# Expert weights in the memory of the mixed values, the second attention's weights loaded beside the routing, and new positions for its parts

## What is computed

```python
x = x + 0.5 * L0_ffn(layernorm(x))     # 8 small experts, every token through all, weights of the best 2
x = x + L0_attn(layernorm(x))          # 32 heads of 32, then a layernorm of its output
x = x + 0.5 * L0_ffn(layernorm(x))
x = x + 0.5 * L1_ffn(layernorm(x))     # 8 large experts, each takes its best 640 tokens (routing by rank)
x = x + L1_attn(layernorm(x))          # 16 heads of 64, with biases
x = x + 0.5 * L1_ffn(layernorm(x))
```

## Time and profile before

| | us |
|---|---|
| median of 3 runs | 3257.68 (3253.45 to 3260.6) |
| the profiled execution's own time | 3266.09 |
| its span in the trace | 3264.3 |
| PE busy | 2913.5 (89% of the span) |
| DVE busy | 2133.6 (65%) |
| POOL busy | 1748.0 (54%) |
| ACT busy | 1720.8 (53%) |

### The profile page before, as it was taken

How to read it: one execution, slowest core, us unless ns; L and a number is a source line. 1 busy time by engine, 2 the same in 40 slices (tenths; PEclk the granted TensorE clock), 3 DMA queues, 4 the chain that set the end, 5 groups by cost and what they waited for, 6 DMA issues and landing times. The chain is left out here.

```text
span 3264.3 us, 46697 instructions
## 1 busy us (share of the span) xinstructions
PE 2913.5 (89%) x16106; PEld 1945.8 (60%) x16106; DVE 2133.6 (65%) x4522; ACT 1720.8 (53%) x3308; POOL 1748.0 (54%) x1540
## 2 busy tenths in 40 slices
PE   7999999999999999989936759999999999998176
PEld 7984565555555555478825736656656566565175
DVE  5667776777777677657765337676676766766632
ACT  5656776767777676757612314444444444443033
POOL 0006988889898888911104714444444444444066
PEclk9999999999999999999967969999999999999588
DMA  2004433434443343300002344344443444432034
GB/s 94 1 20 98 98 88 90 98 80 97 93 93 89 81 97 87 77 5 21 21 30 60 64 114 111 89 104 96 101 104 89 103 93 101 102 89 57 26 76 76
DMA packets 182988, 254.00 MB, mean 78 GB/s; under 512 B 35904, under 2 KB 75584, under 8 KB 182208
## 3 DMA queue, kind: packets, MB, share of 16 engines
q1 hardware_dynamic: 168672, 240.19, 31.1%
q0 software_dynamic: 14080, 10.82, 2.5%
HBM read 33.44 MB, written 16.67 MB: 15 GB/s over the span
## 5 line engine op out<-in xcount | busy, mean ns | idle before, releaser
L1761 POOL TENSOR_TENSOR arena<-arena 128x512 f32<-128x512 f32 x1152 | 1443.5, 1280 | 767.3 <-ACT arena L1132 743.7
L789 PE MATMUL psum<-stack 96*128 96x512 f32 (+4 forms) x4096 | 1247.3, 434 | 37.1 <-DVE top L1391 15.5
L1132 ACT ACTIVATE arena<-psum 128x512 f32<-128x512 f32 x1536 | 854.7, 599 | 604.9 <-PE psum L789 600.4
L1391 DVE TENSOR_REDUCE top<-psum 128x1 f32<-128x512 f32 x1536 | 981.8, 677 | 171.8 <-PE psum L789 169.5
L789 PEld LDWEIGHTS psum<-stack 96*128 96x128 f32 (+4 forms) x4096 | 716.3, 191 | 440.3 <-issue 217.8
L819 PE MATMUL psum<-arena,values 128*32 128x512 f32 (+1 forms) x3072 | 493.3, 598 | 0.5
L819 PEld LDWEIGHTS psum<-arena,values 128*32 128x32 f32 (+1 forms) x3072 | 132.3, 119 | 271.6 <-issue 230.5
L777 PE MATMUL psum<-xT,wqkv 128*128 128x512 f32 x512 | 270.4, 610 | 5.7 <-ACT xT L981 5.7
L1730 POOL TENSOR_SCALAR rstd<-mv 128x4 f32<-128x4 f32 x56 | 12.7, 227 | 473.1 <-DVE mv L1253 471.1
L1422 DVE RECIPROCAL psum<-psum 128x128 f32<-128x128 f32 x256 | 243.3, 954 | 18.6 <-PE psum L851 18.6
L689 PE MATMUL psum<-stack 128*128 128x512 f32 x768 | 213.3, 414 | 20.0 <-DVE stack L1290 20.0
(11 more groups left out here) (155 smaller groups left out, 3132.4 us busy)
## 6 DMA issues: line engine op xcount, KB each, us to landing
stack<-halves SPq DMA_DIRECT2D x768, 128.0 KB, 2.3
stack<-halves SPq DMA_DIRECT2D x384, 256.0 KB, 4.7
tokens<-xn SPq DMA_DIRECT2D x16, 256.0 KB, 2.5
sums<-X SPq DMA_DIRECT2D x16, 256.0 KB, 2.8
wqkv<-in_wg SPq DMA_DIRECT2D x16, 256.0 KB
wqkv<-in_wu SPq DMA_DIRECT2D x16, 256.0 KB
wqkv<-in_wd SPq DMA_DIRECT2D x16, 256.0 KB
wqkv<-in_w_qkv SPq DMA_DIRECT2D x2, 1536.0 KB, 9.6
```

Source lines behind the costliest of these rows:

```text
L789: ins = T_.matmul(bk, st[0:k, side, slot + h, cols], st[0:k, 1 - side, slot + h, :], start=r == 0, stop=r == len(PARTS[l]) - 1)
L1132: S_.activation(prob[l][tile % N_PROB][:, h, :], psum[:, bank[key], :], ACT.Exp, scale=scale).then_inc(released[bank[key]], 1)
L1391: give(V_.reduce_max(top[i][:, j:j + 1], psum[:, bank[key], :], AX.X), key)
L1761: ins = G_.tensor_tensor(to[:, h, :], old[:, h, :], prob[l][tile % N_PROB][:, h, :], ALU.add)
```

## The change

Four things are edited. (1) `wg`, `wu`, `wd` move from `wqkv` to the last 4096 columns of the arena; to make room there, `hid1` is cut from the same memory as the one-hot tables of `positions`, which are done with when it is first written. (2) `load_attention(1)` goes ahead of `experts1(0)` and waits for the last product of the second `experts0`. (3) `experts1(s)` loads its first weights when the attention's last `out` is through. (4) Positions in `WHEN` change, most of them for attention 1.

```diff
@@ WHEN @@
-    dict(project=(-0.11, 0.70), maxima=(0.97, 1.84), rows=(1.94, 1.94), probs=(2.25, 3.17), last=(3.25, 3.37),
-         mix=(3.94, 4.55), out=(4.53, 5.01), ahead=(-2.32, -0.75), finish=(4.91, 4.91), settle=(5.57, 5.86)),
-    dict(project=(-0.11, 0.54), maxima=(1.02, 1.60), rows=(1.80, 1.80), probs=(2.32, 3.28), last=(3.18, 3.47),
-         mix=(3.94, 4.52), out=(4.63, 5.17), ahead=(-2.45, -0.80), route=(5.19, 6.90), ranks=(6.90, 7.60), keep=(8.11, 8.11)))
+    dict(project=(-0.11, 0.70), maxima=(0.97, 1.84), rows=(1.95, 1.95), probs=(2.25, 3.17), last=(3.25, 3.37),
+         mix=(3.94, 4.55), out=(4.53, 5.01), ahead=(-2.30, -0.75), finish=(4.91, 4.91), settle=(5.57, 5.86)),
+    dict(project=(-0.13, 0.59), maxima=(1.02, 1.60), rows=(1.80, 1.80), probs=(2.33, 3.28), last=(3.18, 3.47),
+         mix=(3.90, 4.48), out=(4.58, 4.87), ahead=(-2.46, -0.81), route=(5.11, 6.82), ranks=(6.79, 7.47),
+         keep=(8.06, 8.06)))
@@ attention(l, at) @@
-        stream("load_attention", (l,), 1, 1, at - GROUPS, at - GROUPS)
+        if l == 0:
+            stream("load_attention", (l,), 1, 1, at - GROUPS, at - GROUPS)
@@ program_order @@
-    order.append(("experts1", 0))
-    stream("fold", (), 1, 1, -GROUPS, -GROUPS)
+    order.extend([("load_attention", 1), ("experts1", 0), ("fold",)])
     attention(1, 0)
@@ arena @@
+        here = carve.at
         row_hot = carve(2 * TILES, SLOT_ROWS).bitcast(bf16).rearrange("p j (x r) -> p j x r", x=2)
         within_hot = [carve(16, P // 2).bitcast(bf16) for _ in range(2)]
+        carve = Carve(here)
+        hid1 = [carve(HID1 // P, CAP) for _ in range(2)]
...
-        hid1 = [carve(HID1 // P, CAP) for _ in range(2)]
         rows_out = [carve(SLOT_TILES, DIM) for _ in range(2)]
+        assert carve.at <= ARENA - GROUPS * SEQ
+        carve = Carve(ARENA - GROUPS * SEQ)
+        wg, wu, wd = (carve(2, HID1) for _ in range(3))
         assert carve.at <= KEEP
-        wg, wu, wd = (wqkv[:, i * 2 * HID1:(i + 1) * 2 * HID1].rearrange("p (e f) -> p e f", e=2) for i in range(3))
@@ load_attention(l) on SP @@
                 if l:
-                    sp.wait_ge(*written(("narrow", 0, EXPERTS - 1, 1)))
+                    sp.wait_ge(*written(("down", 1, BATCHES - 1, EXPERTS - 1)))
                     sp.wait_ge(*written(("out", 0, BATCHES - 1)))
@@ experts1(s) on SP @@
-                if s:
-                    sp.wait_ge(*last_value(1, BATCHES - 1))
-                else:
-                    sp.wait_ge(*written(("down", 1, BATCHES - 1, EXPERTS - 1)))
+                sp.wait_ge(*written(("out", s, BATCHES - 1)))
```

## The result

| kernel | median, us | runs | ratio to the kernel before |
|---|---|---|---|
| before | 3257.25 (3253.45 to 3260.6) | 4 | |
| changed | 3223.72 (3219.68 to 3225.83) | 4 | 0.9896 [0.9879, 0.9913] |

The change takes 33.5 us off, 1.0%. The changed kernel's profiled execution took 3225.83 us, with a span of 3224.0.

What follows compares the result with a forecast made beforehand. PE was taken to set the pace inside the attentions, with gains only where it stands still: the entry into attention 1 and its batch ends. 3257.7 less 16 and 7 gave 3234.7, rounded to 3235 us; range 3220 to 3246.

Steps and rivals of the forecast that it cites:

- the forecast's own case: Whole kernel: a time of 3225 to 3243 us, given a chance of 0.70.
- entry: Start of attention 1: the first batch's statistics wait for x alone, no longer for wout; 16.0 us gained, 14 to 17.
- batch ends: Four rounds at each of seven batch ends of attention 1: 7 us gained in all, ends -9 and +35.
- two signs of being wrong: Attention 1's new profile: plain rounds change at all, or the fourth batch-end round moves by more than 1 us.
- Cost of loading earlier: Search in the first experts1: 2 MB ahead delay the first expert weights by 5.5 to 6 us, hidden, costing nothing.
- plain rounds: Attention 1 away from batch ends: PE's order unchanged, later maxima hold nothing up, rounds stay at 15.2 us.
- attention 0: Moved calls of ahead and rows in every batch: no effect, within 1 us over the stage either way.
- (a): First two batch-end rounds: out in two blocks instead of six saves changes of operation, 0.4 us a batch.
- (b): Third batch-end round: an earlier turn shortens PE's 0.7 us wait for the copy of xT, 0.4 us a batch.
- (c): Fourth batch-end round: three comparisons move behind the first reciprocal on DVE; -1 to +1 us, taken as +0.2 a batch.
- third rival: Batch ends: all four comparisons run into POOL's additions, 9 us more than before, 3245 us in all; chance 0.12.
- first rival: Attention 1's batch ends: DVE keeps up, PE never waits, its clock stays high; 3200 to 3220 us, chance 0.10.

Runs made afterwards that it cites:

- a_memory: Changed kernel with the whole WHEN table of the kernel before, so only the memory and load edits; 3250.72 us, ratio 0.9948 to the kernel before.
- h_out_early: Changed kernel with out at (4.53, 4.82) instead of (4.58, 4.87), which moved only its beginning; 3234.84 us, ratio 0.9897 to the kernel before.
- d_old_out: Changed kernel with out back at its former positions (4.63, 5.17) in attention 1; 3229.98 us, ratio 0.9881 to the kernel before.
- k_out_block: Changed kernel with out at (4.57, 4.69), one block of 64 instructions that ends earlier; 3231.82 us, ratio 0.9891 to the kernel before.
- c_old_route: Changed kernel with the former positions of route, ranks and keep in attention 1; 3244.96 us, ratio 0.9927 to the kernel before.
- i_old_ranks: Changed kernel with ranks alone back at its old place (6.90, 7.60); 3237.63 us, ratio 0.9903 to the kernel before.
- g_ranks_gap: Changed kernel with ranks at (6.96, 7.455), meant for the pause between POOL's additions; 3244.83 us, ratio 0.9923 to the kernel before.
- j_ranks_early: Changed kernel with ranks at (6.68, 7.47), meant to run ahead of POOL's additions; 3227.68 us, ratio 0.9882 to the kernel before.
- e_old_mix: Changed kernel with mix back at its old place (3.94, 4.52); 3242.63 us, ratio 0.9922 to the kernel before.

## Why the prediction came out as it did

The time was inside my range, and 11 us below the forecast of 3235; with 3223.7 it lies 1 us under the forecast's own case. The entry earned its part of that. The batch ends did not: their gain was two and a half times what I had, made up of items that I had wrong in both directions, and the total stayed in the range because that had been drawn wide for the rivals. Of my two signs of being wrong, the second came true: the fourth round moved by more than 1 us (19.10 to 16.84 in the mean).

**Entry: right.** 16.0 us predicted, 17.1 seen in the traces, 17.6 by a_memory. From the issue of the first reload to the statistics it is 19.06 us before and 2.97 after, 16.1 less; the other 1.0 us is that the last transfer of expert rows was issued that much earlier in this execution. `fold` went where I had put it, and took half the time, at the high clock; that gained nothing, because it lay under cover.

**Cost of loading earlier, memory, plain rounds: right; attention 0: not told apart.** 5.5 us in the search against 5.5 to 6, hidden; plain rounds unchanged. From its first turn of maxima to its last, attention 0 took 1108.4 us before and 1106.8 in a_memory, with the old positions, and 1105.3 to 1111.4 in the kernels with the new ones, where the two ends are two profiles of the changed kernel itself. An effect within 1 us, as I forecast, can't be seen in that.

**Batch ends: mechanism in part, size wrong.** Predicted 7 us (-2.8, -2.8 and -1.4 for the three items), measured 17.6. The items apart, with the low clock taken out of the fourth round (18.22 us in the mean of six batches at 18.50 and the seventh at 16.53):

- (a) `out` in two blocks: I wrote "I take a third, 0.4 us a batch" of gain. It is a loss of 0.55, 3.9 us in all. I had priced only the changes of operation on PE (which h_out_early shows to be worth nothing), and not the bank that the last block holds until DVE has added it to X, while the next q projection stands right behind. d_old_out and k_out_block show it.
- (b) The copy of xT: 0.4 us predicted, 0.8 measured, 5.6 us in all. The whole wait went, not half of it; c_old_route and i_old_ranks put it on `route`.
- (c) The fourth round: the step that failed is "between -1 and +1. I take +0.2". It is 1.38 us at the high clock, 9.7 us in all. From the earlier trace rows I took one comparison at 1.47 us and one at 0.41, and didn't look at the two between them, which took 1.50 and 1.04. So I took for an exception what was the normal state: before, the ranking already ran into POOL (5.0 us for its six instructions), and the new positions made that less, not more (4.3). The third rival had the right mechanism with the wrong sign.
- The clock: 17.6 us less the 5.6 and 9.7 gained and plus the 3.9 lost leaves 6.2 us. They are the five stretches at the low clock, some 1.2 us each, which vanished as the waits became fewer and shorter. How many there are depends on the execution as well (a_memory, with the old positions, had three), so this item is the least certain. I had this only as a bound and in the first rival, at 0.10; the batch ends went a good way toward that rival.

**What stays open.** The two profiled executions differ by 40.3 us where the medians differ by 33.5. The first turn of attention 1 comes 17.4 us earlier and the way to its last is 18.3 us shorter, 35.7 together; another 4.5 lie in the second `experts1` (277.9 and 273.4 us from the last turn to the end), where only the place of the weights and what their first load waits for were changed. a_memory took 277.4 there, and a second profile of the changed kernel itself 280.1, so this varies from one execution and chip to the next, and I count it for nothing. The search and experts of the first `experts1` vary likewise: from the first load of `wg` to the last addition of rows they took 212.0 us in the first profile of the changed kernel and 218.8 in the second, 218.3 before. So a difference of two single profiles is no measure of the whole; the medians and the rounds are.

## What to carry to other kernels

Before an instruction is moved in a full queue, read the duration of each one of its kind in that stretch, not a median or the first: where one is three times its usual length, look at what the neighbouring engine does then, and move it out of that work. Then read in the new trace where it landed: the place that was worked out for a pause missed it here. When work is gathered into one block, ask who needs the bank that its end holds, and how soon. The end of a block can count where its beginning doesn't.

## What the runs showed of the hardware

Where an operation of DVE with two SBUF inputs and one of POOL meet, one of them takes up to 1.2 us longer, even an instruction of 0.17 us (L1515, 1.12 in g_ranks_gap), and it can be on either side (L1737, 1.81 instead of 1.04 in j_ranks_early). A comparison of 0.41 us took up to 1.57. Not every one beside a row of additions was hit: in the changed kernel L1276 (2378.24 to 2378.65) took 0.41 us while POOL went from one addition to the next, and it was the addition that took 1.49 us.

PE's clock can fall right behind two short waits. In the kernel before, from the fourth round of a batch:

```profile
2140.58 0.74 PE L789 MATMUL psum<-stack 128*128 128x512 f32 x2 [0.52 <-DVE top L1391]
2142.09 1.54 PE L789 MATMUL psum<-stack 128*128 128x512 f32 x4 [0.77 <-DVE top L1391]
```

The low level, 1.2 GHz, was granted from 2142.8 for 3.4 us. In another batch of the same execution the waits were the same, 0.52 and 0.77 us at 2412.67 and 2414.18, and the clock stayed at 2.4 GHz. In g_ranks_gap a drop came in every second batch, in rounds of 19.4 to 19.6 us beside 18.2, so one cost 1.2 to 1.4 us. In the nine kernels whose fourth rounds stayed under 17.7 us there was none in the batch ends of attention 1; they had at most one wait for a maximum at a batch end, the longest of 0.8 us too (c_old_route and i_old_ranks, 4.5 us in six). The kernels with falls had two in nearly every batch (13 in all in the kernel before, a_memory and e_old_mix, 11 in g_ranks_gap). So removing one of two short waits was worth more than its length here. What decides in which batch the clock falls stays open.
